# A graph network kernel on one core: P kept as three bf16 planes and gathered as rows of 768 bytes, in place of fp32 rows of 512 bytes

## What is computed

```python
edge = jnp.concatenate([x[source], x[target], edge_feat], axis=-1)
h = jax.nn.relu(edge @ W1 + b1)
h = jax.nn.relu(h @ W2 + b2)
message = h @ W3 + b3
msum = jax.ops.segment_sum(message, target, num_segments=n)
update = msum / jnp.maximum(cnt, 1.0)[:, None]
return x + update
```

## Time and profile before

| | us |
|---|---|
| median of 3 executions (8710.34 to 8749.07) | 8728.35 |
| the profiled execution | 8749.09 |
| its span, first to last instruction | 8747.3 |
| stage D within it, 2764 to 8690 | 5926 |

### The profile page before, as it was taken

The page is one execution under the profiler, slowest core; times in us unless marked ns, Lnnn a source line. Parts: engine busy times, 40 slices in busy tenths (PEclk is TensorE's granted clock), DMA queues, the critical chain, the costliest instruction groups (busy, mean ns, idle before and its releaser), DMA issues. The chain is left out here.

```text
span 8747.3 us, 164250 instructions
## 1 busy us (share of the span) xinstructions
PE 6514.3 (74%) x48758; PEld 5334.3 (61%) x48759; DVE 3421.8 (39%) x8798; ACT 1878.1 (21%) x3660; POOL 3510.4 (40%) x3525
## 2 busy tenths in 40 slices
PE   4759999999986676667777777667777776767767
PEld 3637887887775555555555555555555555555556
DVE  9988888888833111111112112112111211211112
ACT  1235555555512111111111111111111111111111
POOL 4530001001113454545455555544545455454544
PEclk9999999999985777877777777777777777777777
DMA  5026777777643222222222222222222222222222
GB/s 125 0 88 238 254 251 236 255 252 240 235 146 86 55 57 54 57 55 57 55 55 56 56 57 56 55 55 55 56 56 57 56 57 55 56 56 53 58 55 47
DMA packets 506753, 853.01 MB, mean 98 GB/s; under 512 B 277228, under 2 KB 306126, under 8 KB 506278
## 3 DMA queue, kind: packets, MB, share of 16 engines
q1 hardware_dynamic: 401687, 640.85, 23.3%
q0 software_dynamic: 104960, 210.78, 9.5%
HBM read 579.37 MB, written 271.78 MB: 97 GB/s over the span
## 5 line engine op out<-in xcount | busy, mean ns | idle before, releaser
L1332 POOL DMA_INDIRECT p_got<-p_tab,idx_d x3136 | 2968.9, 947 | 2931.3 <-DMA ef<-in_edge_t 1276.5
L1299 PEld LDWEIGHTS z<-ident_f,p_got 128*128 128x128 f32 x6272 | 1060.5, 232 | 1075.3 <-issue 1063.1
L1318 ACT ACTIVATE h<-z,b_col 128x512 f32<-128x512 f32 x784 | 538.8, 687 | 5085.7 <-remote 3283.3
L1322 DVE TENSOR_TENSOR h<-z,nb 128x512 f32<-128x512 f32 x784 | 540.9, 690 | 2614.4 <-remote 1632.1
L1299 PE MATMUL z<-ident_f,p_got 128*128 128x128 f32 x6272 | 1123.3, 319 | 497.9 <-issue 487.1
L790 PE MATMUL a_ps<-tile_r,pair_l 128*128 128x288 bf16 x6272 | 1229.5, 292 | 181.9 <-issue 86.6
L808 PE MATMUL out_ps<-gw,a_got 121*128 121x144 bf16 x14256 | 1295.7, 227 | 35.8 <-DVE big L855 21.9
L841 DVE TENSOR_SCALAR tile_r<-iota_r,key_r,dst_i 128x576 bf16<-128x576 f16 x3136 | 1170.5, 428 | 281.2 <-PE a_ps L790 135.1
L1311 PE MATMUL seg_ps<-hot_d,h 128*128 128x32 f32 x6272 | 906.6, 281 | 495.8 <-issue 444.3
L1294 PE MATMUL z<-ef,w1c_sb 128*128 128x512 f32 x1568 | 1096.2, 777 | 178.5 <-issue 157.1
L1304 PEld LDWEIGHTS z<-w_sb,h 128*128 128x128 f32 x6272 | 996.2, 224 | 360.2 <-issue 205.5
(11 more groups left out here) (165 smaller groups left out, 3658.5 us busy)
## 6 DMA issues: line engine op xcount, KB each, us to landing
a_got<-a_tab SPq DMA_DIRECT2D x396, 576.0 KB, 4.0
a_tab<-stage SPq DMA_DIRECT2D x392, 576.0 KB
rel<-rel_row SPq DMA_DIRECT2D x392, 192.0 KB
p_got<-p_tab,idx_d POOLq DMA_INDIRECT x3136
ef<-in_edge_t SPq DMA_DIRECT2D x392, 64.0 KB
q_win<-q_tab SPq DMA_DIRECT2D x784, 24.0 KB
a_tab<-big SPq DMA_DIRECT2D x22, 567.0 KB
q_tab<-q_out SPq DMA_DIRECT2D x14, 672.0 KB, 4.7
```

The costliest lines, as they stand in the source:

```text
L1299: pe.matmul(out_tile, p_rows[:, j, :], ident_f[:, :], start=False, stop=False, skip_group_check=True)
L1318: return act.activation(h1[:, :], z1[:, :], ACT.Relu, bias=b1_col[:, 0:1])
L1322: return dve.tensor_tensor(h2[:, :, :], z2[:, :, :], nb2[:, :].unsqueeze(1).to_broadcast([P, GROUP, H]), ALU.max)
L1332: pool.indirect_dma_start(p_rows[:, j, :], None, p_tab, bass.IndirectOffsetOnAxis(idx[:, j:j + 1], 0)).then_inc(landed, 16)
```

## The change

P is split into three bf16 planes as Q is. In stage C, P and Q are rounded and subtracted together, in one tile `pq_out`; the separate fp32 copy of P goes. The table `p_tab` has rows of 768 bytes. In stage D each gather fetches 128 such rows, the buffers `p_got` are four in place of eight, with the wait at L1431 moved accordingly (`z1_made` at least q - 3), and `src_part` adds P's rows by twelve bf16 products in place of four fp32 ones. The extra stage for windows that overflow, which this input does not enter, has its scratch views cut from the new buffers. The core of the diff:

```diff
-    p_tab = dram("p_tab", [NPP, H], F32)
+    p_tab = dram("p_tab", [NPP, PLANES * H], BF16)
...
-            p_out = [sb(f"p_out{k}", [P, CB, H], F32, ctx) for k in range(2)]
-            q_out = [sb(f"q_out{k}", [P, CB, PLANES, H], BF16, ctx) for k in range(2)]
+            pq_out = [sb(f"pq_out{k}", [P, CB, 2, PLANES, H], BF16, ctx) for k in range(2)]
...
-                    if m == 0:
-                        act.copy(p_out[o][:, :, :], v[:, :, 0:H])
-                    act.copy(q_out[o][:, :, m, :], v[:, :, H:2 * H]).then_inc(plane_ready, 1)
+                    act.copy(pq_out[o][:, :, :, m, :], v.rearrange("p b (t h) -> p b t h", t=2)).then_inc(plane_ready, 1)
...
-                    dve.tensor_tensor(rest[:, :, H:2 * H], v[:, :, H:2 * H], q_out[o][:, :, m, :], ALU.subtract
+                    left = rest[:, :, :].rearrange("p b (t h) -> p b t h", t=2)
+                    dve.tensor_tensor(left, v.rearrange("p b (t h) -> p b t h", t=2), pq_out[o][:, :, :, m, :], ALU.subtract
                                       ).then_inc(rest_ready, 1)
...
-                pe.matmul(out_tile, p_rows[:, j, :], ident_f[:, :], start=False, stop=False, skip_group_check=True)
+                for m in range(PLANES):
+                    pe.matmul(out_tile, p_rows[:, j, m * H:(m + 1) * H], ident_b[:, :], start=False, stop=False,
+                              skip_group_check=True)
...
-            p_got = [sb(f"p_got{s}", [P, GROUP, H], F32, life) for s in range(DEPTH)]
+            p_got = [sb(f"p_got{s}", [P, GROUP, PLANES * H], BF16, life) for s in range(UNROLL)]
...
-                        wait_past(pool, z1_made, q - (DEPTH - 1))
+                        wait_past(pool, z1_made, q - (UNROLL - 1))
                         pool.sem_inc(pool_turns, 1)
-                        gather(pool, p_got[s], half_of(idx[s // 2], s), gathered[s])
+                        gather(pool, p_got[s % UNROLL], half_of(idx[s // 2], s), gathered[s])
```

More of the change, by code:

```diff
@@ L406, in _ @@
                 sp.dma_start(q_tab[NP:NPP, :], zero_b[:, :]).then_inc(g_saved, 16)
[L407 removed]
+                sp.dma_start(p_tab[NP:NPP, :], zero_b[:, :]).then_inc(g_saved, 16)
                 for n, (a, z) in enumerate(PARTS):
@@ L1014, in turn @@
                         sp.sem_inc(turns, 1)
-                        sp.dma_start(node_view(p_tab)[:, blocks(n), :], p_out[o][:, :, :]).then_inc(stored[o], 16)
+                        sp.dma_start(node_view(p_tab)[:, blocks(n), :],
+                                     pq_out[o][:, :, 0, :, :].rearrange("p b k h -> p b (k h)")).then_inc(stored[o], 16)
                         sp.dma_start(node_view(q_tab)[:, blocks(n), :],
-                                     q_out[o][:, :, :, :].rearrange("p b k h -> p b (k h)")).then_inc(stored[o], 16)
+                                     pq_out[o][:, :, 1, :, :].rearrange("p b k h -> p b (k h)")).then_inc(stored[o], 16)
                 lagged(sp, NK - 2, DEEP + 2, turn)
@@ L1342, in build_gnn @@
             ef = [sb(f"ef{j}", [P, 2 * W], F32, life) for j in range(PAIRS)]
-            p_got = [sb(f"p_got{s}", [P, GROUP, H], F32, life) for s in range(DEPTH)]
+            p_got = [sb(f"p_got{s}", [P, GROUP, PLANES * H], BF16, life) for s in range(UNROLL)]
+            p_flat = [p[:, :, :].rearrange("p j e -> p (j e)") for p in p_got]
             q_win = [sb(f"q_win{s}", [QR, H], BF16, life) for s in range(DEPTH)]
@@ L1354, in build_gnn @@
             q_x = sb("q_x", [P, PLANES * H], BF16, life)
-            hot_x = p_got[3][:, 0:GROUP // 2, :].rearrange("p j e -> p (j e)").bitcast(BF16).rearrange("p (j e) -> p j e", j=GROUP)
-            hot_xf = p_got[1]
-            hot_xt = p_got[2][:, 0:GROUP // 2, :].rearrange("p j e -> p (j e)").bitcast(BF16)
+            hot_x = p_flat[3][:, 0:W].rearrange("p (j e) -> p j e", j=GROUP)
+            hot_xf = p_flat[1][:, 0:2 * W].bitcast(F32).rearrange("p (j e) -> p j e", j=GROUP)
+            hot_xt = p_flat[2][:, 0:W]
             z1 = [ps(f"z1_{k}", [H, W], F32, life) for k in range(2)]
@@ L1459, in first @@
                         pe.wait_ge(gathered[s], slot_count(q, s, 16 * GROUP))
-                        src_part(pe, z1[k], p_got[s])
+                        src_part(pe, z1[k], p_got[s % UNROLL])
                         pe.wait_ge(hot_t_ready, q + 1)
```

## The result

The changed kernel took 7833.33 us (median of 4, 7827.43 to 7836.81) where the kernel before took 8734.94 (8710.34 to 8749.07) on the same chip: a ratio of 0.897, with a 95% interval of 0.896 to 0.899. It is faster by 10.3%. The forecast was 7991 us, 8.5% faster, with a range from 7550 to 8950. The profiled execution has a span of 7825.6 us.

A forecast was written before the change was run, and what follows sets the result against it. Bound: stage D's long gather runs starve PE of instructions. From the profiled 8749 us, -752 for stage D and +15 for stage C give 8012, and the median 21 lower, 7991 us; range 7550 to 8950.

The forecast's parts named there:

- What bounds the kernel before: Stage D: gather runs of more than some 7 starve PE of instructions until the run ends; 7.56 us a group.
- Four buffers: POOL's wait at L1431 in stage D: runs can't grow to 16 gathers; 6.6 us a group, stage D -752 us.
- the cold cycle: Stage D, two groups started at PE's lower clock: second release at 5.6 us, PE free at 12.1, cycle 13.3 to 14.4.
- The beginning and end of the slow stretch: Stage D: PE slows 7 to 8 us into a gather run, until about 1.5 us behind the last gather.
- the rival of pauses too short: Stage D: pauses of 2.3 to 3.3 us don't restore PE's allowance; 7.2 us a group, median 8462 us; chance 0.22.
- PE, L1299: Stage D's twelve bf16 pairs take 0.66 to 1.09 us, taken as 0.88; the group stays at 4.04 us.
- PE, count: Stage D: 35 pairs a group, not 31, so the slow stretch begins after 1.74 groups in place of 1.97.
- the rival of loads that still gate: Stage D: loads still gate POOL, runs stay 11.6 gathers; +311 and -157 us, median 8897 us; chance 0.12.
- POOL: Stage D: row width doesn't set POOL's time; 1.25 us a gather, other end 1.33, which adds 235 us.
- The rival of a longer gather: Stage D: 768-byte rows cost 1.87 us a gather, 8.4 us a group, median 9400 us; chance 0.10.
- Stage C: DVE's subtraction goes from 1.09 to about 2.2 us, and PE waits for it: +15 us, at most 30.
- What would show it: Profile signs in stage D: idle POOL released by z1, runs of 8, no 12-us slow stretch, clock above 0.76.

The follow-up runs named there:

- 27 pairs: The changed kernel with only plane 0 of P added in src_part (four bf16 products a group, not twelve): 7674.25 us, ratio 0.876.
- the gate of eight: Kernel before with its wait at q - 7 kept; the run there swapped four fp32 products for twelve bf16 ones, rows 512 bytes: 8868.67 us, ratio 1.011.
- the gate of four: Kernel before with only POOL's wait at L1431 moved from q - 7 to q - 3, fp32 rows and eight buffers kept: 7759.96 us, ratio 0.885.
- The gate of seven: Kernel before with only POOL's wait at L1431 moved from q - 7 to q - 6, run on the third chip: 6625.64 us, ratio 1.000.
- the first eight experiments: Eight runs, each with edits to the kernel before or the changed one, on two chips; the kernel before took 8760.88 us and 8602.96 us beside them.

## Why the prediction was right, and where not

*What bounds the kernel before* (runs of gathers that starve PE): right, and stronger than said. Without gathers the group costs the 4.05 us of the earlier trace rows. But "starves PE of instructions" was too narrow. ACT's waits for `z1` in the kernel before and in the changed one (us of idle time, times), over the whole span:

```profile
L1318 ACT ACTIVATE h<-z,b_col x784: 687/687/690, 2774.3 to 8690.9; 128x512 f32<-128x512 f32 x196
its engine sat idle before it (us, times) until:
  remote: 3283.3, 287
```

```profile
L1319 ACT ACTIVATE h<-z,b_col x784: 687/687/691, 2788.1 to 7769.3; 128x512 f32<-128x512 f32 x196
its engine sat idle before it (us, times) until:
  remote: 2819.4, 387
```

Signals are late for ACT and POOL, and not only PE's own instructions. The rows for this stood in the trace of before: I read PE's timeline and never laid ACT's start beside the end of its `z1`.

*Four buffers*, the term that decides: forecast 6.6 us a group, bounds 6.1 and 7.2; measured 6.37 by the window, -934 us where -752 was forecast. The cycle of two groups was put at 12.55 us from a full clock and 13.85 from a cold one. In the trace, runs of eight begin at 5000.78 and 5013.19, 12.41 us apart, though PE entered the first at a clock of 0.77 (the first row below). The step that was mis-sized is the cold cycle: I let PE's speed set it, with "second release at 5.6" and the rest of a group to be done after the slow stretch. In truth a `z1` is finished in only 101 of the 522 pauses. The length of a pause behind eight gathers is that of the hold-up, whatever PE does: 2.4 us in the median here and 2.3 with 27 pairs. The mean, 2 x 6.37 = 12.7, is made up of runs of eight, 12.5 us from start to start, and runs of four, 6.5. That the forecast came as near as 2% is in part luck: its pause of 2.3 to 3.3 us was to be PE's time for the rest of a group, and 2.4 came out for another reason.

*The beginning and end of the slow stretch*: forecast 7 to 8 us into a run, and 1.5 us behind the last gather. Two windows of the changed kernel, cut at a run's start and at PE's slow stretch (columns as in the earlier trace rows):

```profile
5000.80:5008.80 8.00, 8.00 (x59) 6.32 (x57) 1.46 (x5) 0.95 (x3) 6.17 (x7) 0.77 0.37 99
5008.80:5012.20 3.40, 0.82 (x6) 0.80 (x5) 0.00 (x0) 0.00 (x0) 1.38 (x2) 0.87 0.32 85
```

59 matmuls in 8.0 us, then 6 in 3.4, and full pace again at 5012.2, 1.7 us behind the last gather. The beginning held; the end came 0.2 us later than the 1.5 us beyond which the forecast was to be wrong, which changes little. Whether a number of instructions or a time runs out is not settled: the fall comes 8 to 9 us into a run, and with 27 pairs a group, which put fewer matmuls into it, about 1 us later. A pause of 2.4 us restored the whole allowance, so the rival of pauses too short (8462 us) fell. The pauses that I had quoted were of 5.9 us and more, and told nothing of short ones.

*PE, L1299*: 12 pairs took 5007.63 - 5006.96 = 0.67 us at the full clock, 0.056 each: the lower bound of 0.66 and not the middle, 0.88. The figure of 81 ns that I quoted from the Trainium skill (TensorE: Matmul & The Clock Gate, Back-to-back issue gap) for such a stream is not borne out here; what the same section gives for a matmul by itself, 56 ns at 128 columns, is what the trace has. The row with 512 columns was the one to go by. It was of little use in the end: what PE saves, it mostly waits.

*PE, count*: four pairs more cost 1.1%, 94 us of 8761 (108 by the medians), at the gate of eight. For that case the rival of loads that still gate had 311 - 157 = +154 us; the direction was right, the size 1.4 to 1.6 times too large.

*POOL*: 0.949 us a gather and a pitch of 1.25, as taken. (The 8300 us given for 1.33 us a gather do not come out of its term: 7991 + 235 is 8226.) The rival of a longer gather (9400 us) had no ground. *Loads still gate*: `ef` is POOL's releaser once in stage D, at its start; it fell too. *Stage C*: forecast +15; the first `z1` came 12.5 us later, and DVE's subtraction takes 2.02 us where it took 1.09:

```profile
2663.25 2.02 DVE L1197 TENSOR_TENSOR rest<-pq_ps,pq_out 128x1792 f32<-128x1792 f32 x1 [1.27 <-ACT pq_out L1037]
```

*The clock*: forecast above 0.76 in D, measured 0.79.

*What would show it* named "POOL's idle time in D released by L1466" and "runs of 8 gathers". The first is 138 us by name, and 666 us are "remote", late signals of the same line; the second holds for 248 of 522 runs, and most of the rest are of 4.

The forecast was thus right in its decisive term for half its reason: the gate of four does keep POOL from running 16 gathers ahead. But half the runs were of eight already, and their pause was 6 us in the median where it is 2.4 now: the larger gain is that a pause no longer contains a load's 4.7 us, which the forecast named (as 4.6) but did not give as what is gained. The change's own idea, bf16 planes, is a small loss beside it. The kernel before with q - 5 or q - 3 at L1431 is faster than the kernel before on the chips with the hold-up, and by the ratios at least as good as the changed one: 0.891 and 0.885, each on its own chip, against 0.897. It never ran beside the changed kernel on one chip, where a difference of 1% could be told.

What stays open: why two chips of three, and the one of the main comparison, hold signals up behind a run of gathers, and the third does not. That it is the chip, and not something else that differed there, is not shown either; the record names only the chip. The gate of seven did not run on a chip with the hold-up, so where between six and eight the step lies is open too. The gathers' own busy time in D is the same on both kinds (2969 and 2978 us). The changed kernel did not run on the third chip. By the mechanism it should be near the kernel before there, since POOL's gathers alone set 5.03 us a group; that is argued, not shown.

## What to carry to other kernels

Where a consumer starts microseconds after its producer ended, and the profile says "issue" or "remote", lay the two timelines beside each other before costing any instruction: a saving on the engine that seems to be the bound may count for little, as eight pairs of 35 did here (2%). When a change alters a wait along with the data, run the wait alone; here one number gave the whole gain. And compare on the same chip, on more than one: the same program took 6625 us on one and 8761 on another, and what gains 11% on one kind has nothing to gain on the other, where POOL never pauses.

## What the hardware did that I had not expected

- On the chips of the main comparison and of the first eight experiments, some 8 us into a run of back-to-back indirect DMAs of 128 rows, PE falls from 7 matmuls a microsecond to 0.6, and signals from PE to ACT and POOL are seen late, one `z1` in ten by some 16 us or more in the kernel before. It ends some 2 us after the last gather. The width of a row plays no part (192, 512 and 768 bytes).
- On the third chip 3136 such gathers in a row, at the same 1.25 us, delay nothing: not one `z1` was seen later than 0.8 us.
- A pause of 2.4 to 2.7 us behind 10 us of gathers is enough to bring back the full allowance: 59 matmuls in the next 8 us.
- Pairs of weight load and bf16 matmul of 128 columns follow each other in 56 ns at the full clock.
